# A transformer decoder block with routed experts: 128-slot tiles whose tokens stand still, expert weights split once and kept in memory, and expert outputs added in memory

## What is computed

```
x = layernorm(x + self_attention(x))            # 16 heads, rotary positions, causal
x = layernorm(x + cross_attention(x, ctx, mask))# 1601 context rows per sequence, one head of width 512
x = layernorm(x + routed(x) + shared(x))
# shared(x) = silu(x @ wg.T) * (x @ wu.T) @ wd.T          with wg, wu 256x512, wd 512x256
# scores = sigmoid(x @ gate_w.T)                          2048 x 16
# topk = 4 experts of the largest scores + bias; weights = their scores, normalised to sum 1
# routed(x) = sum over the 4 chosen experts e of weight_e * expert_e(x), expert_e built like shared
```

## Time and profile before

| | |
|---|---|
| three timed executions | 1553.42, 1556.15, 1558.72 us |
| the profiled execution, whole | 1543.42 us |
| its span, first to last instruction | 1541.7 us |
| granted TensorE clock, mean | 0.943 of full speed |
| TensorE busy | 1375.3 us (89%) |
| VectorE, ScalarE, GpSimd busy | 1017.8, 789.6, 340.5 us |
| moved by DMA | 190.37 MB |

### The profile page before, as it was taken

How to read it: one execution, slowest core, us unless ns; L and a number is a source line. 1 busy time by engine, 2 the same in 40 slices (tenths; PEclk the granted TensorE clock), 3 DMA queues, 4 the chain that set the end, 5 groups by cost and what they waited for, 6 DMA issues and landing times. The chain is left out here.

```text
span 1541.7 us, 25128 instructions
## 1 busy us (share of the span) xinstructions
PE 1375.3 (89%) x8837; PEld 1148.1 (74%) x8837; DVE 1017.8 (66%) x1685; ACT 789.6 (51%) x1545; POOL 340.5 (22%) x490
## 2 busy tenths in 40 slices
PE   5899999999998589999999865899999999998990
PEld 5667766766774378888888654899999999997770
DVE  6667676676675564646554378677777777773777
ACT  4777577577576242424233242566566656653222
POOL 0243233234222210100100001222222222222662
PEclk9999999999998789999999985899999999998995
DMA  4200000000000240413220040777788778884563
GB/s 177 110 1 28 1 1 29 1 1 1 1 1 1 87 149 1 128 43 107 65 84 25 2 150 10 270 280 278 287 289 286 273 283 280 284 282 148 168 189 138
DMA packets 62029, 190.37 MB, mean 123 GB/s; under 512 B 7161, under 2 KB 7165, under 8 KB 61185
## 3 DMA queue, kind: packets, MB, share of 16 engines
q1 hardware_dynamic: 49312, 147.93, 26.6%
q0 software_dynamic: 12640, 41.43, 9.0%
HBM read 156.30 MB, written 33.03 MB: 123 GB/s over the span
## 5 line engine op out<-in xcount | busy, mean ns | idle before, releaser
L436 PE MATMUL proj_ps<-wqkv,x_sp 128*128 128x384 f32 x768 | 172.9, 355 | 10.2 <-DVE wqkv L315 10.2
L1549 DVE TENSOR_TENSOR e_w_sp<-e_w_raw,e_w_sp 128x1024 fp32r<-128x1024 f32 x141 | 168.8, 1222 | 18.2 <-ACT e_w_sp L1507 11.5
L1493 POOL DMA_INDIRECT e_x_g<-x_rows,e_index x94 | 101.6, 1080 | 323.0 <-DVE e_index L1560 308.4
L1006 PE MATMUL c_score_ps<-ct,x_t 128*128 128x402 f32 x768 | 160.1, 361 | 0.0
L1507 ACT ACTIVATE e_w_sp<-e_w_raw 128x1024 fp32r<-128x1024 f32 x141 | 145.6, 1058 | 16.1 <-DMA e_w_raw<-w_experts 15.8
L1025 PE MATMUL c_out_ps<-cr,weigh_t 128*128 128x512 f32 (+1 forms) x624 | 147.3, 394 | 1.4 <-DVE weigh_t L865 1.4
L1006 PEld LDWEIGHTS c_score_ps<-ct,x_t 128*128 128x128 f32 x768 | 141.4, 194 | 7.2 <-issue 5.3
L1608 PEld LDWEIGHTS e_gate_ps<-e_x_t,e_w_sp 128*128 128x128 f32 x1128 | 140.5, 191 | 5.9 <-DVE e_x_t L1570 1.8
L1608 PE MATMUL e_gate_ps<-e_x_t,e_w_sp 128*128 128x256 f32 x1128 | 142.1, 282 | 1.4 <-DVE e_x_t L1570 1.4
L1608 PE MATMUL e_up_ps<-e_x_t,e_w_sp 128*128 128x256 f32 x1128 | 143.3, 283 | 0.0
L436 PEld LDWEIGHTS proj_ps<-wqkv,x_sp 128*128 128x128 f32 x768 | 131.7, 194 | 11.6 <-issue 10.1
(11 more groups left out here) (212 smaller groups left out, 2377.5 us busy)
## 6 DMA issues: line engine op xcount, KB each, us to landing
e_w_raw<-w_experts SPq DMA_DIRECT2D x141, 512.0 KB, 5.6
y_rows<-e_y SPq DMA_DIRECT2D x47, 512.0 KB
raw<-ctxT SPq DMA_DIRECT2D x16, 800.5 KB, 4.3
raw<-ctx_rows SPq DMA_DIRECT2D x16, 768.0 KB, 4.8
rows<-x_rows SPq DMA_DIRECT2D x1, 4096.0 KB, 12.2
x_rows<-rows SPq DMA_DIRECT2D x4, 1024.0 KB, 5.9
out<-rows SPq DMA_DIRECT2D x4, 1024.0 KB, 5.2
rows<-wqkvT SPq DMA_DIRECT2D x4, 768.0 KB, 7.4
```

The source lines that it names most:

```text
L436: mm = nc.tensor.matmul(proj_ps[:, tt, 0:GW], x_sp[:, xs, c, tt * P:(tt + 1) * P], wqkv[:, ws, c, hg * GW:(hg + 1) * GW], start=(c == 0 an ...
L1006: mm = nc.tensor.matmul(score_ps[:, f, 0:MQ], x1_t[:, xs, c, qt * P:(qt + 1) * P], ct[:, cs, c, f * MQ:(f + 1) * MQ], start=False, stop=(c ...
L1493: nc.gpsimd.indirect_dma_start(x_g[:, par, half, :], None, x2_rows, bass.IndirectOffsetOnAxis(ap=index[:, par, half:half + 1], axis=0)).th ...
L1549: nc.vector.tensor_tensor(w_sp[:, par, part, 1, :], w_raw[:, par, part, :], w_sp[:, par, part, 0, :].bitcast(F32), ALU.subtract).then_inc( ...
```

## The change

**Cross attention.** 13 of the 16 experts are split in advance here, in 104 pieces of 384 columns (8 an expert). SP fetches a piece (`fetch`, 192 KB) in one of `NB` = 4 buffers, ScalarE writes its high part (`hi_piece`), VectorE its low part (`lo_piece`), and SP stores both to the new tensor `w_split` (`store`, 384 KB). `PIECES_OF` says how many are put between and behind the transposes of a tile: 0 and 4, 4 and 5, 4 and 0, 4 and 5 for the four tiles of a sequence. A store, and the fetch behind it, wait in SP's queue, into which the context loads are woven. The mask row has one buffer in place of two and is added last in the first tile of a sequence.

**Routing.** The other 24 pieces are split here. The shared expert moves here from combine, with its matmuls woven into the marks, and with its low parts made by GpSimd. Its result is added to `rows`, which are stored to memory (`acc[0]`); `acc[1]` is filled with zeros. `x2_rows` gets 16 more columns, the token's weight for each expert. `line_up` works out in some thirty small VectorE instructions the order of the experts, after how many tiles each buffer is free, and each tile's buffer.

**Routed experts.** `SLOTS` is 128 and `TILES` 79. There is no loop, all 79 tiles are written out. SP loads both parts of an expert's weights once (3 MB, 24 KB in a row for each partition) into one of `RING` = 4 buffers. In the products the tokens are the standing operand and the weights the columns. A tile has 12 + 6 matmuls of 512 columns, 4 + 2 transposes, and two register loads for the number of experts that must be there and for the buffer. GpSimd gathers tile m+4 and then adds the weighted rows of tile m to memory with an indirect DMA that adds (`scatter`), into `acc[m % 2]`.

**End.** `finish_rows` takes combine's place: it loads `acc[0]` and `acc[1]`, adds them, normalises and stores.

```diff
-SLOTS = 2 * P
+SLOTS = P
 TILES = (NT * P * TOPK + E * (SLOTS - 1)) // SLOTS
+SPLIT_EARLY = 13
+PIECE = 384
+PIECES = WE // PIECE
+NB = 4
+RING = 4
...
 def cross_attention(...):
+        PIECES_OF = {0: (0, 4), 1: (4, 5), 2: (4, 0), 3: (4, 5)}
...
+                def fetch(g):
+                    if g >= NB:
+                        sp.wait_ge(piece_out[g % NB], 16 * (g // NB))
...
+                def store(g):
+                    sp.wait_ge(piece_lo, g + 1)
+                    at = g % PIECES * PIECE
+                    sp.dma_start(w_split[g // PIECES, :, :, at:at + PIECE], piece[:, g % NB, :, :].bitcast(F32)
+                                 ).then_inc(piece_out[g % NB], 16)
+                def pieces(first, last):
+                    for g in range(first, last):
+                        store(g)
+                        if g >= 1 and g - 1 + NB < first_piece[NT]:
+                            fetch(g - 1 + NB)
...
+                for slot in range(NB):
+                    sp.wait_ge(piece_out[slot], 16 * (first_piece[NT] // NB))
...
 def route(...):
+                front(0, 0)
+                front(0, 1)
                 rank()
-                for t in range(NT):
-                    mark(t)
+                front(1, 0)
+                front(1, 1)
+                for t in range(BEFORE_ADDS):
+                    mark(t)
+                back(0, BEFORE_ADDS, TT)
+                front(2, 0, BEFORE_ADDS + TT, 2)
+                front(2, 1, BEFORE_ADDS + TT + 4, 2)
+                back(1, BEHIND_UP, NT - BEHIND_UP)
+                front(3, 0)
+                front(3, 1)
+                back(2)
+                back(3)
...
 def routed_experts(...):
+                def gather(m):
+                    if m >= XG:
+                        pool.wait_ge(x_turned, m - XG + 1)
+                        pool.wait_ge(weight_set, m - XG + 1)
...
+                def scatter(m):
+                    if m >= 2:
+                        pool.wait_ge(*added(m - 2))
+                    pool.wait_ge(y_done, m + 1)
+                    nc.gpsimd.indirect_dma_start(
+                        acc[m % 2], bass.IndirectOffsetOnAxis(ap=token_row[:, 1, m:m + 1], axis=0),
+                        y[:, m % YB, :], None, compute_op=ALU.add
+                    ).then_inc(y_added[m % 2], 16)
...
+                def weigh_y(m):
+                    act.wait_ge(down_done, m + 2)
+                    act.wait_ge(weighed, m + 1)
+                    if m >= YB:
+                        act.wait_ge(*added(m - YB))
...
+                for m in range(TILES):
+                    needed, slot = place(m)
+                    front(m, needed, slot)
+                    if m >= 1:
+                        back(m - 1, before)
+                    if m + 2 < TILES:
+                        turn_x(m + 2)
+                    turn_h(m)
+                    before = slot
...
-def combine(nc, sem, rows, w_sp, y_rows, plan, out):
+def finish_rows(nc, sem, rows, acc, out):
...
+                for b in range(B):
+                    dve.wait_ge(row_in[b], 32)
+                    for t in range(b * TT, (b + 1) * TT):
+                        nc.vector.tensor_tensor(rows[:, t, :], rows[:, t, :], odd_rows[:, t, :], ALU.add
+                                                ).then_inc(summed, 1)
```

More of the change, by code:

```diff
@@ L837, in tile @@
                         exponentials(n + 1)
+                    for k in range(behind):
+                        hi_piece(g + between + k)
                     if qt == TT - 2 and b + 1 < B:
@@ L936, in tile @@
                             lo_context(b + 1, c)
+                    for k in range(behind):
+                        lo_piece(g + between + k)
                     if n in LATE_NORMS:
@@ L1177, in _ @@
+                silu(3)
+                hi_h(3)
+                for g in range(BEHIND_PLAN):
+                    hi_piece(FIRST_PIECE + IN_MARKS + BEHIND_PLAN + g)
             @block.vector
@@ L1442, in routed_experts, with added, gathered @@
+        y_added = [sem(f"e_y_added{par}") for par in range(2)]
+        weight_set, weighed = sem("e_weight_set"), sem("e_weighed")
+        def added(m):
+            return y_added[m % 2], 16 * (m // 2 + 1)
+        def gathered(m):
+            return x_in[m % XG], 16 * (m // XG + 1)
         with nc.Block() as block:
@@ L1475, in _, with tell @@
+                def tell(n):
+                    sp.wait_ge(w_in[n % RING], 16 * (n // RING + 1))
+                    sp.sem_inc(loaded, 1)
+                for n in range(RING):
+                    load(n)
+                for n in range(RING):
+                    tell(n)
+                for n in range(RING, E):
+                    load(n)
+                    tell(n)
                 for par in range(2):
-                    sp.wait_ge(y_stored[par], 16 * ((TILES + 1 - par) // 2))
+                    sp.wait_ge(y_added[par], 16 * ((TILES + 1 - par) // 2))
@@ new lines, in place, with weights, front @@
+                def place(m):
+                    return (pe.value_load(needed_at[0:1, m:m + 1], min_val=1, max_val=E),
+                            pe.value_load(slot_at[0:1, m:m + 1], min_val=0, max_val=RING - 1))
+                def weights(slot, part, first, last):
+                    return w[:, bass.ds(slot, 1), part, first:last].rearrange("p o n -> p (o n)")
+                def front(m, needed, slot):
+                    pe.wait_ge(x_lo, m + 1)
+                    pe.wait_ge(loaded, needed)
+                    if m >= 2:
+                        pe.wait_ge(h_done, m - 1)
+                    for c in range(DC):
+                        for n, (xs, ws) in enumerate(PASSES):
+                            mm = nc.tensor.matmul(both_ps[:, m % 2, :], x_t[:, m % 2, xs, c * P:(c + 1) * P],
+                                                  weights(slot, ws, c * GU, (c + 1) * GU),
+                                                  start=(c == 0 and n == 0), stop=(c == DC - 1 and n == 2))
+                    mm.then_inc(both_done, 1)
@@ L1677, in combine @@
[L1677 to L1683 removed]
+        odd_rows = ctx.enter_context(nc.sbuf_tensor("odd_rows", [P, NT, D], F32))
@@ L1685, in combine @@
+        row_in = [sem(f"f_row_in{b}") for b in range(B)]
+        summed, stored = sem("f_summed"), sem("f_stored")
         with nc.Block() as block:
@@ L1688, in _ @@
             def _(sp):
+                for b in range(B):
+                    for dst, src in ((rows, acc[0]), (odd_rows, acc[1])):
+                        sp.dma_start(dst[:, b * TT:(b + 1) * TT, :],
+                                     src[b * T:(b + 1) * T, :].rearrange("(t p) d -> p t d", p=P)
+                                     ).then_inc(row_in[b], 16)
                 for b in range(B):
```

1036 lines of the change are left out of this document (542 added, 494 removed).

## The result

The change made the kernel slower: 1624.12 us median (1616.41 to 1625.24) against 1555.33 beside it, ratio 1.0429 with the interval 1.0397 to 1.0461. The profiled execution took 1616.41 us, its span 1614.3. Forecast were 1524 us and, as likelier than not, a gain.

The account below looks back on a forecast made before the run. TensorE was taken to bound cross attention and experts, VectorE's chain routing, and gathers and adds the last stage's tail. Terms 8 + 55 - 12 - 83 = -32 gave 1511 us, carried to the median 1524 us; range 1485 to 1600.

Parts of the forecast that it names:

- tile of 5.15 us: Routed experts: 4.86 us of TensorE work plus about 0.3 us of uncovered register loads per tile, 407 us in all.
- about 0.3 us is left: Routed experts: TensorE's sequencer runs ahead, so of some 0.9 us of register loads only about 0.3 us stays uncovered.
- the second rival: Routed experts: register loads on TensorE are exposed, 5.7 us a tile, 1568 us (fully exposed 6.6 and 1640); chance 0.11.
- later loads are short beside the slack: Routed experts: weight loads delay memory adds only in the first 40 us, 12 us in all; later ones cost nothing.
- the first rival: Routed experts: memory adds set the pace; at 12.2 us landing a tile takes 6.8 us, 1640 us; chance 0.17.
- start of 12.5 us: Routed experts: the wait for the first weights, 3 MB at 377 GB/s plus a landing of 3.8, 12.5 us.
- Cross attention, +8: Cross attention: only the last tile's nine pieces lack cover, needing about 20 us against TensorE's 12; 8 us longer.
- upper bound of +30: Cross attention: if the ring's waits reach the softmax chain, eight tiles of nine pieces lose some 4 us each.
- it just fits: Cross attention: 13 pieces through the ring of four take 39.7 us against 41.3 us of TensorE work in two tiles.
- Routing, +55: Routing: after the scores TensorE's 80 us, 8 us of waits and a 5.2 us store; 55 us longer, bounds +44 and +80.
- End, -83: Last stage: VectorE sets the pace at 7.1 us a quarter, 45 us against 127.7; bounds -88 and -75.
- two signs of being wrong: Changed profile: the forecast is wrong if expert fronts are over 5.6 us apart or routing takes over 150 us.

Follow-up runs that it names:

- run 13: Changed kernel with gathers eight tiles ahead and the slots and needed loads of two tiles (four values) in one register load; ratio 0.9962 to the kernel before.
- Run 4: Changed kernel with tokens' rows gathered eight tiles ahead instead of four (ring of eight buffers); ratio 1.0168 to the kernel before.
- run 5: Changed kernel with constants instead of TensorE's register loads and gathers eight tiles ahead; ratio 0.9943 to the kernel before.
- run 7: Changed kernel with no weight pieces fetched, split or stored, experts taking unsplit weights (low part wrong); ratio 1.0192 to the kernel before.

## Why the prediction was wrong

Of the 105 us between the forecast's -32 and the measured +73, the experts hold 64, cross attention 22, routing 20, and the end 1 of the other sign.

- **Experts, tile of 5.15 us: the step on the sequencer failed.** The work was sized well (18 x 0.234 + 6 x 0.11 = 4.86; with constants 4.80 was measured) and so were the loads (0.9 against 0.95 us). Wrong was "about 0.3 us is left": 0.68 was. The step took from one instruction near a matmul's start that the loads begin 0.9 us before the array is done; only 0.27 us of them ran under other work. That is 0.33 x 79 = 26 us, the second rival's mechanism at 5.48 us a tile, between the forecast and its 5.7. The Trainium skill ("DMA: Bandwidth & Descriptors", section "Latency and other measured facts") puts such a load at 600 ns at least. This case's traces disagree: on TensorE it took 306 ns for one value and 336 for four (run 13), and the median is above 600 only for eight values and more.
- **Experts, "later loads are short beside the slack": failed.** The slack was counted for the adds (four output buffers). But gather m+4 stands on GpSimd behind add m-1, which waits for add m-3, and TensorE wants it two tiles later. Landings of 9.4 and 10.3 us beside a load, of which the text had the size (12.2), were enough, at nearly every load and not in the first 40 us only. With the lower clock behind eight of the ten stalls 44 us, not 12: 32 of the 64. Run 4 shows that it was this slack; the first rival's pace of two adds was not the limit at 5.48 us a tile, and appears only at 4.8 (run 5).
- **Experts, start of 12.5 us:** 17.7, since the first gathers landed while four weight loads ran (TensorE waited for `e_x_g` until 1072.57 and again until 1076.77). With these 5 it is 63 of the 64. (The forecast's own terms, 3 MB at 377 GB/s and 3.8, make 12.1.)
- **Cross attention, +8: the tail was right in kind, the cover was not.** 10.9 us of the 30 are the last tile (31.6 us from its exponentials to routing against 20.8 before), where 8 were forecast. The other 19 (22 less the 3 by which the first read-out starts earlier) lie in eight of the fifteen stretches from one read-out to the next, 1.8 to 4.1 us each, where TensorE waits at L1071 for VectorE (15.9 us in eight waits). The pace of 2.3 us was right, and the text had a loss of this kind as its upper bound of +30. The step that failed is "it just fits", which set the ring against TensorE's work alone. ScalarE, VectorE and SP also load and split the next sequence's context in their lists, and six of the eight stretches are those in which they do so, beside four or five pieces. In the last sequence, with no next context, the stretches of eight and nine pieces are only 0.2 and 0.1 us longer than before, though ScalarE waits 3.5 and 5.3 us for fetches in them. That it is this meeting is read from the stretches and not from a run of its own. About 1.5 us in three of the six is there without any pieces too (run 7).
- **Routing, +55: near without its pieces** (125.4 us measured, 129 forecast with them). The pieces were to lie under TensorE's work, and 8 us were put for all waits; they cost 24 us. The step that failed took VectorE's 72 us as a sum beside TensorE's 80, and left out that SP's stores and fetches stand behind VectorE's long stretch on the plan. The event at 1017 to 1040 us above shows it, with the low clock behind it.
- **End, -83:** -84.5 measured. VectorE's pace and the last store were the right terms.

Of what was to be seen, the 43 us at the end came, and GpSimd did idle for `e_y` (236.3 us against 27.9 for the adds). Routing was past its 140, cross attention past its 15, the fronts past 5.3 us apart and the landing beside a load past 9 us. But neither of the two signs of being wrong came (fronts over 5.6 us apart, routing over 150): they were 5.5 and 149.0. Those signs looked at an undisturbed tile, and so missed the stalls. Four covers were priced one by one, each as if its neighbours were on time. A range to 1600 left out that several could fail together, as they did.

## What to carry to other kernels

A prefetch's distance counts from where its issue really stands: behind which waiting instruction of the same queue, and what that one waits for. Here four more buffers took out all but 1 of 44 us of stalls. A register load in a matmul engine's stream was paid mostly in the open here (0.68 of 0.95 us), and constants or one packed load for one or two tiles were worth 0.5 to 0.7 us a tile. And a ring whose mean pace fits can still cost what it hides, if engines with other work stand in its order: take away its transfers and its arithmetic in turn, and see whether the cost is a load or a meeting of two. Count also what else those engines serve in the same stretch.

## What the runs showed of the hardware

- An indirect transfer that adds in memory holds GpSimd 1587 ns, one that only writes 990, and a gather of the same 128 rows 987.
- Beside rows of 24 KB a 128-row gather landed 9.4 us after its issue and an add 10.3. With the same bytes in rows of 3 KB the stalls were 18 us instead of 44, in rows of 12 KB 51 to 58.
- After 2.84 us in which TensorE was idle the next front took 4.61 us instead of 3.03 (granted clock 0.63); after 18.6 and 3.1 us at the stage's start 5.48 us, at 0.50, the lower of its two clocks throughout. The idle time alone doesn't tell: behind 2.01 us (until 1189.04) the front took 5.48 us at 0.50, behind 2.10 us (until 1142.38) 3.06 at 1.00.
- TensorE's register load took 306 ns for one value, 541 for two, 336 and 492 for four, 644 for eight and 1290 for sixteen.
